# A mixture-of-experts block on one core: one indirect transfer in nine split into four of 32 rows

## What is computed

```python
logits = x_flat @ W_router
probs = jax.nn.sigmoid(logits)
topk_probs, topk_idx = jax.lax.top_k(probs, TOPK)
topk_probs = topk_probs / (jnp.sum(topk_probs, axis=-1, keepdims=True) + 1e-06)
combine = jnp.zeros((N, E)).at[jnp.arange(N)[:, None], topk_idx].add(topk_probs)
out = sq_relu(x_flat @ W_sh_up) @ W_sh_down
for e in range(E):
    h = sq_relu(x_flat @ W_up[e])
    out = out + combine[:, e:e + 1] * (h @ W_down[e])
...
x = x + attn(xn, ...) + ffn(xn, ...)
```

## Time and profile before

| | |
|---|---|
| median of 3 runs | 476.17 us (476.06 to 481.84) |
| profiled execution | 475.49 us, span 473.7 us, mean granted clock 0.989 |
| TensorE matmul busy | 430.6 us (91%) |
| VectorE busy | 347.7 us (73%) |
| ScalarE busy | 293.8 us (62%) |
| GpSimd busy | 158.6 us (33%) |
| scatters, first to last start | 64, 83.1 to 198.8 us |
| gathers, first to last start | 64, 349.4 to 464.7 us |

### The profile page before, as it was taken

The page is one execution under the profiler, slowest core; times in us unless marked ns, Lnnn a source line. Parts: engine busy times, 40 slices in busy tenths (PEclk is TensorE's granted clock), DMA queues, the critical chain, the costliest instruction groups (busy, mean ns, idle before and its releaser), DMA issues.

```text
span 473.7 us, 12356 instructions
## 1 busy us (share of the span) xinstructions
PE 430.6 (91%) x4354; PEld 340.8 (72%) x4355; DVE 347.7 (73%) x684; ACT 293.8 (62%) x514; POOL 158.6 (33%) x186
## 2 busy tenths in 40 slices
PE   8889678899989999969999999999998998989995
PEld 8778346556566666659999999999965665655664
DVE  8977877788879777855665665665657989988833
ACT  1444446658767765846656666666665766776682
POOL 5270004645655565500000000000034654654562
PEclk9999889999999999989999999999999999999999
DMA  8482202333333452345455445554132342342131
GB/s 230 149 367 79 80 3 69 123 111 124 107 104 104 161 169 85 102 134 151 151 139 156 148 140 148 155 144 122 46 90 73 111 129 78 116 135 71 41 93 44
DMA packets 64177, 56.61 MB, mean 120 GB/s; under 512 B 6658, under 2 KB 56324, under 8 KB 63620
## 3 DMA queue, kind: packets, MB, share of 16 engines
q1 hardware_dynamic: 59364, 42.49, 29.6%
q0 software_dynamic: 4096, 8.40, 6.2%
q10 hardware_dynamic: 672, 5.11, 2.6%
HBM read 26.61 MB, written 16.52 MB: 91 GB/s over the span
## 4 chain that ended last, share of the span: by engine, by line
PE 75%; DVE 17%; issue 5%; ACT 2%; DMA 1%; DVEq 0%; POOL 0%; POOLq 0%; ACTq 0%; SPq 0%
PE pbank L1383 15%; PE sbank L1263 13%; PE obank L1238 9%; DVE maxes L938 8%; PE fbank L1181 5%; PE fbank L1070 3%; PE tbank L1070 3%; PE fbank L1071 3%; PE fbank L1072 3%; PE tbank L1072 2%; PE tbank L1071 2%; PE sbank L1375 2%; PE wbank L1217 2%; PE pbank L1070 2%; PE wbank L1070 1%
## 5 line engine op out<-in xcount | busy, mean ns | idle before, releaser
L938 DVE TENSOR_REDUCE maxes<-sbank 128x4 f32<-128x1024 f32 x128 | 156.6, 1223 | 50.2 <-PE sbank L1263 48.0
L697 ACT ACTIVATE probs<-tbank 128x1024 f32<-128x1024 f32 x128 | 130.9, 1023 | 84.3 <-PE tbank L1268 81.5
L508 POOL DMA_INDIRECT gathered<-results,place_of x64 | 60.9, 951 | 199.4 <-PE tbank L1268 193.3
L1263 PE MATMUL sbank<-k_bands,q_bands 31*128 31x256 f32 x512 | 64.8, 329 | 26.5 <-DVE maxes L938 19.4
L1263 PEld LDWEIGHTS sbank<-k_bands,q_bands 31*128 31x128 f32 x512 | 39.1, 185 | 63.9 <-DVE maxes L938 41.9
L499 POOL DMA_INDIRECT slots<-X,place_of x64 | 61.7, 965 | 50.3 <-PE tbank L1268 46.9
L1383 PE MATMUL pbank<-down_w,probs 128*128 x624 | 76.1, 275 | 0.6 <-ACT gathered L745 0.6
L1383 PEld LDWEIGHTS pbank<-down_w,probs 128*128 128x128 f32 x624 | 72.7, 192 | 0.7 <-issue 0.7
L1238 PE MATMUL obank<-probs,v_ones 128*32 128x256 f32 x1024 | 70.3, 393 | 0.0
L1268 PE MATMUL tbank<-q_bands,k_bands 32*128 32x256 f32 x512 | 64.9, 331 | 0.6 <-ACT probs L697 0.6
L1041 DVE TENSOR_TENSOR block_lo<-block_w,block_hi 128x512 fp32r<-128x512 f32 x39 | 27.0, 692 | 47.4 <-ACT block_hi L730 47.3
(11 more groups left out here) (181 smaller groups left out, 827.7 us busy)
## 6 DMA issues: line engine op xcount, KB each, us to landing
block_w<-in_w_up SPq DMA_DIRECT2D x39, 256.0 KB
results<-gathered SPq DMA_DIRECT2D x39, 128.0 KB, 1.9
q_bands<-part_hi SPq DMA_DIRECT2D x32, 128.0 KB
k_bands<-part_hi SPq DMA_DIRECT2D x32, 128.0 KB
slots<-q_bands ACTq DMA_DIRECT2D x1, 4096.0 KB, 11.6
gathered<-slots SPq DMA_DIRECT2D x20, 128.0 KB, 2.1
relu_T<-slots SPq DMA_DIRECT2D x19, 128.0 KB, 2.1
q_bands<-part_lo SPq DMA_DIRECT2D x16, 128.0 KB
```

The lines of the kernel that those rows point to most:

```text
L508: pool.indirect_dma_start(out=gathered[:, c % RING, k * TT + t, :], out_offset=None, in_=results, in_offset=bass.IndirectOffsetOnAxis(ap=p ...
L697: nc.scalar.activation(probs[:, j % 4, :], tbank[:], ACT.Exp, scale=SCALE).then_inc(exps_ready, 1)
L938: nc.vector.tensor_reduce(maxes[:, g // 2, :, 2 * pair:2 * pair + 2, g % 2].rearrange("p t q -> p q t"), sbank[:].rearrange("p (q t k) -> ...
L1263: ins_s = nc.tensor.matmul(sbank[:, (2 * k + t) * T:(2 * k + t + 1) * T], q_bands[q:q + TOP, r1, g, s], k_bands[q:q + TOP, r1, g, :], star ...
```

## The change

The slot with two transfers is given up. A new function `schedule` gives every slot one whole transfer; the ninth (n = 6, 15, 24, ...) is cut into four of 32 partitions, and each is issued right behind the whole one of one of four slots: slots 2 to 5 in the first half, slots 4 to 7 in the second. With 7 groups in each half that makes 28 short scatters and 28 short gathers; the others stay whole. The last gather (n = 63) is still issued behind the loop.

The row numbers of an indirect transfer are taken from partition 0 on, so those of partitions 32 to 127 are first copied to partitions 0 to 31 of a new tile `place_low`, by three small transfers on SyncE's queue in b = 1. GpSimd waits for them (`places_moved`) before each short transfer but the first of a group. Semaphore counts follow: `parts` says how many transfers a batch has; `scattered` becomes four semaphores, and a scatter now waits for the batch four before it. FINAL is computed from the slot of a batch's last part: batches 1, 5, 7 and 10 are added one slot later, batches 3 and 12 two slots later, the others as before.

```diff
-SHARE = (2, 1, 1, 1, 1, 1, 1, 1)
-GATHER = [(b, j) for b in range(ROUTED_AT + 1, B) for j in (0, 1, 2, 3, 3, 4, 5, 6, 7)]
-FINAL = {divmod(max(b * SLOTS + j + 3, (c + 2) * SLOTS), SLOTS): c for c, (b, j) in enumerate(GATHER[3::4])}
+def schedule(first, last):
+    out = {}
+    for s in range(first, last):
+        g, i = divmod(s - first, SLOTS)
+        n = 9 * g + i + i // 6
+        out[divmod(s, SLOTS)] = [(n, None)] + ([(9 * g + 6, i - 4)] if i >= 4 else [])
+    return {s: [(n, q) for n, q in v if n < 4 * B] for s, v in out.items()}
+
+SEND = schedule(FIRST[0] * SLOTS + FIRST[1], (ROUTED_AT + 1) * SLOTS)
+GATHER = schedule((ROUTED_AT + 1) * SLOTS, B * SLOTS)
+
+def parts(c, ring):
+    return sum(4 if n % 9 == 6 else 1 for d in range(c % ring, c + 1, ring) for n in range(4 * d, 4 * d + 4))
+
+LAST_OF = {n // 4: s for s, v in sorted(GATHER.items()) for n, _ in v}
+FINAL = {divmod(max(b * SLOTS + j + 3, (c + 2) * SLOTS), SLOTS): c for c, (b, j) in LAST_OF.items() if c < B - 1}
...
+                if b == FIRST[0]:
+                    sp.wait_ge(places_ready, 2)
+                    for q in range(3):
+                        sp.dma_start(place_low[:, q, :], place_of[32 * q + 32:32 * q + 64].rearrange("p k t -> p (k t)")
+                                     ).then_inc(places_moved, 16)
...
+            def places(k, t, q):
+                if q is None or q == 0:
+                    return bass.IndirectOffsetOnAxis(ap=place_of[0:32 if q == 0 else P, k, t:t + 1], axis=0)
+                pool.wait_ge(places_moved, 48)
+                return bass.IndirectOffsetOnAxis(ap=place_low[:, q - 1, k * TILES + t:k * TILES + t + 1], axis=0)
+
+            def dispatch(n, q):
+                t, k, c, rows_ = n // 2, n % 2, n // 4, rows_of(q)
+                if c >= 4 and c not in sent:
+                    pool.wait_ge(scattered[c % 4], 16 * parts(c - 4, 4))
+                sent.add(c)
+                at = places(k, t, q)
+                pool.indirect_dma_start(out=slots, out_offset=at, in_=X[rows_, t, :], in_offset=None).then_inc(scattered[c % 4], 16)
...
+                    if SEND.get((b, j)) or (b, j) in GATHER:
                         after_scores(b, j)
+                    for n, q in SEND.get((b, j), ()):
+                        dispatch(n, q)
+                    for n, q in GATHER.get((b, j), ()):
+                        collect(n, q)
+            for n in range(9 * (B - ROUTED_AT - 1), 4 * B):
+                collect(n, None)
```

More of the change, by code:

```diff
@@ L131, in build @@
         place_of = sb("place_of", [P, 2, TILES], I32)
+        place_low = sb("place_low", [32, 3, 2 * TILES], I32)
         pair_hi = sb("pair_hi", [P, 2, P], F32R)
@@ L232, in build @@
         places_ready = sem("places_ready")
-        scattered = [sem("scattered0"), sem("scattered1")]
+        places_moved = sem("places_moved")
+        scattered = [sem(f"scattered{c}") for c in range(4)]
         pair_loaded = [sem(f"pair_loaded{c}") for c in range(4)]
@@ L403, in routed @@
             def routed():
-                sp.wait_ge(scattered[0], 16 * TILES)
-                sp.wait_ge(scattered[1], 16 * TILES)
+                for c in range(B - 4, B):
+                    sp.wait_ge(scattered[c % 4], 16 * parts(c, 4))
                 def load(q, slot):
@@ L491, in after_scores, with rows_of, collect @@
                 pool.wait_ge(scores_T_done, b * SLOTS + j + 1)
[L493 to L505, removed]
+            def rows_of(q):
+                return slice(0, P) if q is None else slice(32 * q, 32 * q + 32)
+            def places(k, t, q):
[10 more added lines that the diff above has]
+                pool.indirect_dma_start(out=slots, out_offset=at, in_=X[rows_, t, :], in_offset=None).then_inc(scattered[c % 4], 16)
+            def collect(n, q):
+                c, k, t, rows_ = n // 4, n // 2 % 2, n % 2, rows_of(q)
+                if c >= RING and c not in fetched:
                     pool.wait_ge(batch_final, c - RING + 1)
[L508 to L511, removed]
+                fetched.add(c)
+                at = places(k, c * TT + t, q)
+                pool.indirect_dma_start(out=gathered[rows_, c % RING, k * TT + t, :], out_offset=None, in_=results,
+                                        in_offset=at).then_inc(rows_gathered[c % RING], 16)
             def split(src):
@@ L559, in _ @@
             pool.wait_ge(bias_ready, 1)
-            sent, fetched = 0, 0
+            sent, fetched = set(), set()
             for b in range(B):
@@ L572, in _ @@
                         add_bias(b)
[L573 to L579, removed]
-                        after_scores(b, j)
[L581 to L585, removed]
+                    if SEND.get((b, j)) or (b, j) in GATHER:
+                        after_scores(b, j)
+                    for n, q in SEND.get((b, j), ()):
[4 more added lines that the diff above has]
+                collect(n, None)
         @block.scalar
@@ L978, in add_batch @@
                 if c >= EARLY:
-                    dve.wait_ge(scattered[c % 2], (c // 2 + 1) * 64)
+                    dve.wait_ge(scattered[c % 4], 16 * parts(c, 4))
                 if c < B - 1:
@@ L989, in first_expert @@
                 dve.wait_ge(batch_added, c + 1)
-                dve.wait_ge(rows_gathered[c % RING], (c // RING + 1) * 64)
+                dve.wait_ge(rows_gathered[c % RING], 16 * parts(c, RING))
                 for t in range(TT):
```

## The result

The changed kernel takes 535.06 us (median of 4 runs, 530.20 to 535.97) against 476.81 us for the kernel before (median of 4 runs on the same chip): a ratio of 1.119, 95% interval 1.114 to 1.124. It is 12% slower; 4% were forecast, and the range ended at 514 us.

A forecast was written before the change was run, and what follows sets the result against it. It took TensorE's score signals, made late by second transfers, to bound the kernel: 475.5 - 13.1 removed + 32.7 added (23.1 first half, 9.6 second) = 495.1, median 496 us, 4% slower; range 464 to 514, the forecast's own 486 to 508.

The forecast's parts named there:

- What bounds the kernel, and what holds the signal: VectorE's maxima wait for TensorE's score signal, late while a second transfer is prepared; slot 1 is 1.31 us longer.
- What is removed: Doubles at slot 0 of b = 2 to 8 and slot 3 of b = 9 to 15: 7.9 and 5.2, together 13.1 us.
- The duration d of 32 rows: GpSimd's time for one short transfer: bounds 0.24 and 0.96 us, the middle, 0.60, taken.
- rival 3: A short transfer takes GpSimd as long as a whole one, 0.96 us: median 512 us, far slower; chance 0.12.
- The release at d + 0.63 after the start: Signals falling due during a short transfer come free 0.63 us after its end.
- the formula of the prediction: First-half losses behind short transfers: d + 0.25, d + 0.17, d + 0.14, d + 0.35; 3.3 us an iteration, 23.1 in all.
- Rival 4: GpSimd falls behind and short transfers drift into the next slot; counted inside the forecast, with no chance of its own.
- slack behind a whole transfer: Time from a whole transfer's start to the next maxima, slots 2 to 5, first half: 1.64, 1.72, 1.75, 1.54 us.
- The second half's share of four in seven: In the second half four in seven signals behind short transfers are late: 16 x 0.60 = 9.6 us added.
- The other parts at nothing: Copies to place_low, semaphores and moved closing slots cost near nothing (VectorE pieces -1 to +2 us); expert stage stays 145 us.

The follow-up runs named there:

- without extras: The changed kernel with all 56 short transfers left out, those rows neither sent nor fetched, one whole transfer a slot: 468.83 us, 0.979 of the kernel before.
- halves: The changed kernel with each ninth transfer sent as two of 64 rows instead of four of 32, beside the first and third whole ones: 498.58 us, 1.045.
- double in slot 4: The kernel before with the two-transfer slot moved to slot 4 in both halves, all rows sent, semaphores as in the changed kernel: 484.26 us, 1.012.
- halves ahead of even slots: The changed kernel with two 64-row transfers per ninth one, in slots 3 and 5 (first half), 5 and 7 (second): 499.87 us, 1.045.
- double in slot 5: The kernel before with the two-transfer slot moved to slot 5 in both halves, all rows sent, semaphores as in the changed kernel: 483.26 us, 1.010.

## Why the prediction was wrong, point by point

**What bounds the kernel, and what holds the signal: right.** A second transfer in a slot holds TensorE's signal where that falls due soon after its start; arithmetic in its place does not, and without extras slot 1 takes 1.82. **What is removed: right, somewhat too high**, 13.1 us forecast, 9.4 measured (478.24 - 468.83), 10.8 in the two halves.

**The duration d of 32 rows: wrong, the first failed term.** 0.60 was taken, the middle between 0.24 and 0.96; it is 0.86. Between 0.86, 0.91 (64 rows) and 0.96 (128) a row costs about 1 ns, which leaves an estimated 0.83 us for none. The step's reason, "since no row is nearer to one end", was wrong in itself: rival 3 had named the rows that are nearer. Scatter and gather do different work for a row and take 0.96 and 0.94, as a fixed cost would. The Trainium skill's rule ("DMA: Bandwidth & Descriptors", anatomy of a DMA on the gpsimd path), that many descriptors can be emitted before their cost shows, pointed the same way, and the trace agrees: 0.86 for 32 rows against 0.96 for 128. It deserved more than 0.12. Yet d = 0.86 alone brings the prediction's sum only to 506.7 us (30.5 + 13.8 added), of 535.8 measured: most of the miss lies in the points that follow.

**The release at d + 0.63 after the start: wrong in form, nearly right in size.** In the rows above the signal is free 1.56 to 1.65 after the start of a second transfer with none right behind it, whether it took 0.86, 0.91 or 0.96; the 0.63 behind the end is 0.70 to 0.74 behind a short one. So a shorter transfer lowers the loss hardly at all. It is no constant of the chip: behind second transfers of 1.04 to 1.11 us (halves, slot 4; double in slot 4, first half) it is mostly 1.79 to 1.92, and in a chain it can be earlier (0.88 to 1.02, halves ahead of even slots). With the whole transfer's 1.59 the formula of the prediction gives rival 3's 33.3 us for the first half; 33.1 were measured. The agreement is of the sum, not of the slots, and partly luck: four losses of about 1.2 were to fall in slots 3 to 6, and they fell as 1.2, 0, 2.8 and 0, with 0.9 in slot 7 (3.13, 4.81 and 2.74 us against 1.92 and 2.04 for slots 3 and 5 and the undisturbed 1.82).

**Rival 4, "I expect the slot to stretch rather than GpSimd to lag": wrong.** Both happen in turn. A signal that is due in the first 0.3 us of a transfer can get through (222.11 after; 150.43 with the double in slot 5), the slot doesn't stretch, GpSimd's two transfers (0.96 + 0.30 + 0.86 + 0.30 = 2.42 us) don't fit into its 1.83, and the next slot's transfers join on without a pause. From the start of such a chain to the signal that was held, the rows give 2.85 us for two transfers, 4.70 for three (148.88 to 153.58), 6.35 for four (220.57 to 226.92) and 8.99 for six (158.65 to 167.64): 1.4 to 1.6 for each, more than the 1.16 to 1.27 by which GpSimd's rows are apart. A slot of 1.82 to 2.04 has room for one such and not for two, and none of the slots tried beats those of before. The rows read as if the 1.54 to 1.75 us that I took for slack behind a whole transfer were used up by it.

**The second half's share of four in seven: wrong, the second failed term.** 25.5 us for 24 short ones, 9.6 forecast for 28. For the doubles the reading was fair: from b = 9 to 14 they cost 1.2, 0.0, 1.5, 0.7, 0.0 and 0.8 us an iteration (before against the kernel without extras), though in b = 14, called on time in the earlier trace rows, the loss stood one slot later (slot 5 took 2.93 us before and takes 2.14 without extras). What failed was to carry the share over to short transfers in other slots: in the changed kernel every one of the six iterations is longer than without extras, by 3.1 to 5.5 us. The double was free in b = 10 and 13 for a reason of slot 3. Before, b = 10:

```profile
371.08 0.86 DVE L928 SCALAR_TENSOR_TENSOR part_lo<-pbank,bias,part_hi 128x256 fp32r<-128x256 f32 x2
371.87 1.21 DVE L938 TENSOR_REDUCE maxes<-sbank 128x4 f32<-128x1024 f32 x1
...
372.43 0.95 POOL L508 DMA_INDIRECT gathered<-results,place_of  x1 [0.30 <-issue]
...
373.68 1.23 DVE L938 TENSOR_REDUCE maxes<-sbank 128x4 f32<-128x1024 f32 x1
```

Slot 3 takes 2.97 there with or without a double, because VectorE has `second_expert` (1.11 us) and line 928 (0.86) ahead of its maxima, which then start without a wait. GpSimd's chain has begun meanwhile, and the signal of slot 4 falls due 1.25 after the second transfer's start and is not held. With the double in slot 4 the same iteration loses 1.3 us. So a double is free where its slot is late already; the short ones of slots 4 to 7 had no such slot. Taken with d = 0.86, a release at 1.59, and all late, the formula gives 0.96 each, 23.0 us for the 24, near the 25.5 measured.

**The other parts at nothing: right** for the copies, the semaphores and the expert stage (147.1 us; 147.0 before). **The clock was not in the sum at all.** In the first half its extra cost is small (33.1 us measured for 28 x 1.16 = 32.5 by the transfers' own 0.86 + 0.30), though TensorE is 9.9 us longer busy with the same matmuls. In the end the clock is 0.83, and of the 7.8 us there some 4.6 are the four extras of b = 15 by the same price. The 4.6 us at the start stand before the transfers begin and came in part with a lower clock.

The sum with measured terms: 475.5 - 10.8 (removed, both halves) + 33.1 + 25.5 (added to b = 14) = 523.3. With 4.6 at the start, 7.8 at the end and 0.1 in the expert stage it is 535.8, the profiled execution's own time (span 534.0 and 1.8 around it). All these terms are differences of windows of the same traces, so that they add up is no test. Against the prediction's 495.1 they say where its error lies: 2.3 us in what is removed, 10.0 in the first half's short transfers, 15.9 in the second's (and more in b = 15), 12.5 in what stood at nothing. What stays open: why TensorE's signal is held at all, and which share of the start's and the end's 12 us is the clock's alone. No order of the 64 transfers tried here beats the one before.

## What to carry to other kernels

Count the indirect transfers on GpSimd, not their rows: here one of 32 rows cost what one of 128 did, and each stood for some 1.2 us of the loop once its slot was full. Where an unknown duration must be bounded, ask which rows vary the amount of work and look whether the duration follows; two kinds of work with one duration point to the fixed end. And where a wait vanishes in one slot (slot 1, or those that got through), look at the next two before it is counted as a gain. A share of late signals that was read for one slot is not the share of another: ask first what made the slot late or not.

## What the runs showed of the hardware

- An indirect transfer on GpSimd takes 0.86 us for 32 rows, 0.91 for 64 (1.04 for rows 64 to 127 through place_low) and 0.96 for 128 (up to 1.11 for the second of a double in slot 4), with 0.30 us between two issues.
- TensorE's signals can be held while one is prepared: in the rows shown they are free 1.56 to 1.65 us after the start of the second of two (1.79 to 1.92 where that took 1.04 to 1.11), and 2.85, 4.70, 6.35 and 8.99 us after the start of a chain of two, three, four and six. A signal that fell due 1.25 us after the second's start was not held (373.68 before). GpSimd's arithmetic (0.63 us) holds none: one passed 0.55 us into an addition. TensorE itself stops in the end: at 166.77 above, the last of sixteen matmuls starts 1.03 us after the fifteenth ended, with nothing to wait for in the profile.
- With chains of six transfers the loss seems to come a second time, as clock: after 7 us in which TensorE was busy for 3.30, the granted clock was 0.52 for the next 7 us and the sixteen value matmuls took 1.94 us instead of 1.07; over the half it was 0.84.
